# A preactivation convolution pair on one core: the high and low f16 planes move into one buffer, pixel by pixel side by side

## The reference

```python
x = x + silu(bn(sum_e routing[b, e] * conv3x3(gn(x), w_experts[e])))   # 4 experts, routing = sigmoid(mean(gn(x)) @ w_route.T + b_route)
x = x + conv3x3(gn(x), sign(W))                                       # all weights are -1, 0 or 1
```

## Time and profile before

| | |
|---|---|
| median of three runs | 274.24 us (274.05 to 274.51) |
| the profiled execution | 273.91 us |
| its span in the trace | 272.1 us |
| TensorE busy | 264.7 us, 97% of the span, 1339 matmul records |
| VectorE busy | 256.2 us, 94% |
| ScalarE busy | 219.7 us, 81% |
| GpSimd busy | 54.1 us, 20% |
| granted TensorE clock, mean | 0.998 |

### The profile page before, as it was taken

The page is one execution under the profiler, slowest core; times in us unless marked ns, Lnnn a source line. Parts: engine busy times, 40 slices in busy tenths (PEclk is TensorE's granted clock), DMA queues, the critical chain, the costliest instruction groups (busy, mean ns, idle before and its releaser), DMA issues.

```text
span 272.1 us, 4138 instructions
## 1 busy us (share of the span) xinstructions
PE 264.7 (97%) x1339; PEld 181.9 (67%) x1339; DVE 256.2 (94%) x466; ACT 219.7 (81%) x450; POOL 54.1 (20%) x63
## 2 busy tenths in 40 slices
PE   8899999999999999999999999999999999999993
PEld 7545846768485766859586675848576685958663
DVE  5799999999999999999999999999999999996985
ACT  2489998998969898897989899897989986835870
POOL 3001020312131031414112041413203141210110
PEclk9999999999999999999999999999999999999999
DMA  6988855452715555351645544362555536182407
GB/s 200 416 356 281 316 184 154 73 128 50 136 78 87 147 78 143 57 111 78 111 123 77 154 65 93 90 123 96 81 154 77 122 66 125 77 137 96 77 2 154
DMA packets 10245, 35.20 MB, mean 129 GB/s; under 512 B 1264, under 2 KB 1904, under 8 KB 10224
## 3 DMA queue, kind: packets, MB, share of 16 engines
q0 software_dynamic: 4176, 15.21, 33.1%
q1 hardware_dynamic: 5616, 19.34, 18.7%
q10 hardware_dynamic: 432, 0.39, 0.4%
HBM read 11.34 MB, written 16.25 MB: 101 GB/s over the span
## 4 chain that ended last, share of the span: by engine, by line
PE 92%; DMA 2%; DVE 2%; ACT 1%; SPq 1%; issue 1%; POOL 0%; DVEq 0%
PE pc L590 42%; PE pa L555 15%; PE pb L555 14%; PE pe_ L555 13%; PE pd L545 6%; DMA X<-x 2%; PE ps L524 1%; PE ps L528 1%; PE pa L627 0%; PE pb L627 0%; DVE U L1152 0%; DVE X L1377 0%; ACT hi L929 0%; SPq L408 0%; POOL rstd L441 0%
## 5 line engine op out<-in xcount | busy, mean ns | idle before, releaser
L1162 DVE SCALAR_TENSOR_TENSOR U<-we,route,U 128x1152 f32<-128x1152 f32 x45 | 63.6, 1414 | 0.6
L590 PE MATMUL pc<-hi,ws 128*128 128x496 f16 (+3 forms) x270 | 59.8, 375 | 0.5 <-ACT hi L929 0.5
L590 PE MATMUL pc<-lo,ws 128*128 128x496 f16 (+3 forms) x270 | 59.7, 375 | 0.0
L441 POOL TENSOR_TENSOR rstd<-ve,nhalf 128x2 f32<-128x2 f32 (+1 forms) x19 | 26.6, 1399 | 135.0 <-ACT ve L844 111.3
L590 PEld LDWEIGHTS pc<-hi,ws 128*128 128x128 f16 x270 | 26.4, 98 | 30.0 <-issue 0.9
L590 PEld LDWEIGHTS pc<-lo,ws 128*128 128x128 f16 x270 | 26.5, 102 | 27.8
L555 PE MATMUL pa<-V,UM 128*128 128x256 f32 (+1 forms) x180 | 41.7, 381 | 0.0
L555 PE MATMUL pb<-V,UM 128*128 128x256 f32 (+1 forms) x180 | 40.7, 376 | 0.1
L555 PE MATMUL pe_<-V,U 128*128 128x256 f32 (+1 forms) x180 | 40.6, 375 | 0.0
L555 PEld LDWEIGHTS pb<-V,UM 128*128 128x128 f32 x180 | 34.0, 190 | 5.4 <-issue 0.6
L555 PEld LDWEIGHTS pe_<-V,U 128*128 128x128 f32 x180 | 34.1, 190 | 3.8
(11 more groups left out here) (165 smaller groups left out, 394.8 us busy)
## 6 DMA issues: line engine op xcount, KB each, us to landing
X<-x SPq DMA_DIRECT2D x15, 512.0 KB, 5.6
out<-X SPq DMA_DIRECT2D x15, 512.0 KB, 2.6
out<-ev POOLq DMA_DIRECT2D x15, 512.0 KB, 5.4
X<-y POOLq DMA_DIRECT2D x14, 512.0 KB, 4.5
we<-w_experts SPq DMA_DIRECT2D x2, 768.0 KB, 8.9
ws_raw<-w_sign SPq DMA_DIRECT2D x1, 576.0 KB, 11.5
we<-w_experts SPq DMA_DIRECT2D x1, 512.0 KB, 6.8
out<-X SPq DMA_DIRECT2D x1, 384.0 KB, 2.7
```

The source lines that it names most:

```text
L441: g.tensor_tensor(rstd[:, c, a:b], ve[:, c, a:b], nhalf[:, a:b], ALU.pow).then_inc(rstd_ready, 1)
L590: mm = mm_(rows[:, r0 - first // W:r1 - first // W, c0:c1], ws[:, tap * C:(tap + 1) * C], plane((hi, lo)[part], i)[:, r0 + ky - 1:r1 + ky ...
L1162: v.scalar_tensor_tensor(out=nine(U[i % RING]), in0=expert(e), scalar=route[:, i, e:e + 1], in1=nine(U[i % RING]), op0=ALU.mult, op1=ALU.a ...
```

## The change

The four buffers hi0, hi1, lo0 and lo1 become two, hilo0 and hilo1, of as many pixels and two f16 numbers for each pixel. hi and lo are the first and the second number of each pair. The bytes are as many as before; every instruction, its order, its waits and its number of elements stay. What differs is that each instruction that reads or writes hi or lo now steps by two f16 elements (four bytes) from pixel to pixel, where it stepped by one (two bytes).

```diff
         last_size = LAST_TILES * POINTS * W + LAST_REST * W
-        hi = [sb(f"hi{p}", [C, HW if p != (B - 1) % 2 else last_size], F16) for p in range(2)]
-        lo = [sb(f"lo{p}", [C, HW if p != (B - 1) % 2 else last_size], F16) for p in range(2)]
+        hilo = [sb(f"hilo{p}", [C, HW if p != (B - 1) % 2 else last_size, 2], F16) for p in range(2)]
+        hi = [hilo[p][:, :, 0] for p in range(2)]
+        lo = [hilo[p][:, :, 1] for p in range(2)]
```

## The result

The changed kernel takes 279.38 us (median of four runs, 278.99 to 279.60) against 274.34 us for the kernel before in the same session: a ratio of 1.0187, with an interval of 1.0174 to 1.0199. It is slower, as forecast, but by 5.0 us and not by 112. The case that came true is the second rival, a smaller loss, in its second form: the reading side lost a part.

A forecast was written before the change was run, and what follows sets the result against it. TensorE, without gaps, was taken to bound the kernel. Terms of +108.0 (sign products), +4.3 (last image) and -0.5 us (a vanished wait) made +111.8, forecast 386.0 us; range for eight in ten 273.7 to 390.

The forecast's parts named there:

- the second rival: Slower writes, 286 us at most, or sign products losing part of their pace, 1.1 us per 1%; chance 0.09.
- The bound: Whole kernel: TensorE has no gap, so whatever lengthens a sign product lengthens the 15.60 us step by as much.
- What fits both rows is one word per partition every two cycles: TensorE's operand reads: four bytes every two cycles, inferred from f32 pace and f16 rows of 31 costing as much as 32.
- the upper end: Sign products on TensorE: one column in two cycles, so eighteen take 7.41 us instead of 3.81.
- the term of +108.0 us: Sign products of images 0 to 14: two runs of eighteen per image, each 3.60 us longer.
- The tail: Last image: two slower product runs before the inverse transform, +1.83 us, and VectorE waiting for pe_, +2.5; together +4.3 us.
- The term of -0.5 us: Last image: TensorE's 0.47 us wait for ScalarE's statistics goes, as longer sign products let them come in time.
- The writes: ScalarE writing hi, VectorE writing lo: a four-byte pitch costs nothing; upper estimate each row again, hidden if TensorE slows.
- The cover of 0.36 us: Between ScalarE's end of hi at 113.87 and TensorE's use at 114.23: slack that hides slower writing of hi.
- its 0.31 us of the earlier trace: VectorE's slack in each step: it may grow by 0.31 us before it matters, covering slower writing of lo.
- sign_points: Three VectorE sums using lo may lose their fast form, 0.6 us once, hidden in a 2.73 us wait for pa.
- No change: TensorE's reading side takes any two pixels in one beat, sign products keep their time: 274.2 us; chance 0.26.

The follow-up runs named there:

- the planes apart: Kernel before with 10 KB per partition freed, plus hi and lo each at a four-byte pitch in a buffer of its own: 279.06 us, ratio 1.0179.
- the first of the two programs with single streams: Separate program, no kernel changed: streams of one instruction form at several pitches; 512 f16 columns took 216 ns packed, 226 at 4 bytes, 451 at 8.

## Why the prediction was wrong, by its own steps

**The bound was read rightly.** TensorE sets the step, has no gap, and what a sign product gains in length the step gains 36 times.

**The step that failed** is the one that ends "What fits both rows is one word per partition every two cycles", and with it the choice of the upper end, "a sign product runs at the f32 pace". Two facts of the trace were joined that have nothing to do with each other. The f32 products' pace, two cycles a column, was taken for the pace of memory; it is not, for f16 at the same pitch takes 226 ns (L77) where 512 f32 columns take 429 (L112). A row of 31 f16 pixels does cost as much as one of 32, but two pixels need not lie in one word to come at full pace. In place of words the runs showed lines of 16 bytes, 1.76 ns each. The 18 products touch 12 x 128 + 6 x 120 = 2256 lines (a row of 31 or 32 pixels has 8), 3.97 us, and the chain has 3.98. So the term of +108.0 us measured +5.0. The error would have shown at once if the f32 row had been used as what it was, a bound from above, with nothing in the rows to say how far below it the truth lay; half of the chance and more went to its far end.

**The tail** of +4.3 us hung on the same step.

```profile
268.17 1.01 PE pb L628 x12
269.18 1.03 PE pa L628 x12
...
273.42 0.36 DVE X L1387
```

Here the products of L628 have 48 lines, 84 ns, against 82 to 83 before: two runs of 1.01 and 1.03 us for 0.99 and 1.01. From the start of pb's run to VectorE's last instruction it is 5.25 us for 5.22, and VectorE still sets the end. The term of -0.5 us, which counted on a longer run of sign products, measured -0.1: TensorE's wait for the statistics (L506, at 262.36) is 0.36 us for 0.47.

**The writes** were taken at zero, because f32 neighbours with the same pitch are as fast. That comparison missed that f32 fills its words. A half-word written into a word costs, and each hi took 0.30 us more, each lo 0.16. The cover of 0.36 us from the earlier trace rows was right and held all but some 0.3 us in total. VectorE had its 0.31 us of the earlier trace rows and did not come up.

**sign_points** went as written: three sums slower by 0.2 us, hidden by VectorE's wait for pa, which was 2.10 us (L1238) for 2.73.

**The rivals.** No change, with 0.26, failed by 4%: the reading side does take two pixels from two words in a beat, as that rival had it, but the supply of lines falls just short, 225 ns for 216. The rule that was named beside it, of the Trainium skill, "Advanced Engine Details and Errata", section Memory Cachelines, has the right unit, lines of 16 bytes, and the wrong threshold for this engine at full clock: by it a line needs at least two hits, and, as the prediction read it, two suffice; here four hits cost 4% and two (8 bytes, 451 ns) more than double the time. The measurement decides. The smaller loss came true by its second form: 4.4% on the sign products (3.98 for 3.81 us) at the 1.1 us for each 1% that it gave is 4.9 us. What was missing was a way to size it, and the program with one pitch after another gives it. This case had a chance of 0.09. That the range of 273.7 to 390 holds the measured time is luck: it was stretched down to no change for another rival's sake, and the likeliest case by itself was 382 to 390.

What stays open: lo took 1383 ns in the changed kernel and 1314 with the planes apart, while VectorE alone shows no price for reading and writing halves of the same words (1293, and 1340 for the costliest pattern). The 70 ns lie under cover; their cause was not looked for.

## What to carry to other kernels

Count the 16-byte lines that a moving operand touches and hold 1.76 ns for each against the time of its columns: packed f16 uses half of that supply (64 lines, 113 of 216 ns), a 4-byte pitch slightly more than all of it, and each further byte of pitch up to 16 is paid in full. Interleave by whole lines (rows of 64 bytes cost nothing here), not by elements, and never write half-words where the writer is on the path. When the trace of before does not have an operation, a neighbour with another type bounds its price but does not set it.

## What the runs showed of the hardware that was not expected

The supply of lines does not follow TensorE's clock. In the first of the two programs with single streams, the stretches (us, TensorE busy, granted clock) of L85, of L87 and of the f32 products (L112 to L116) were:

```profile
88.00:104.00 16.00, 16.00 (x25) 0.57 0.00 0
104.00:125.00 21.00, 21.00 (x25) 0.50 0.00 0
...
199.00:242.00 43.00, 43.00 (x76) 1.00 0.00 0
```

At pitches of 12 and 16 bytes the clock was granted at 0.57 and then 0.50 of full, which is 1.2 GHz, though matmuls stood back to back throughout; a line still took 1.76 ns (676 / 384 and 900 / 512). The f32 products at 16 bytes took the same 899 ns a record at the full clock, so the lines come at one pace at either clock. A TensorE that waits for its operand is busy in the profile; in f16 it yet lost its clock at pitches of 12 bytes and more, in f32 at the same price it kept it. Why the two differ was not looked for. Every pixel has a line of its own already at 16 bytes, and at 32 bytes (L89, (147.69 - 125.66) / 24 = 918 ns) the price hardly changes.

A line written in half-words costs 4.4 ns on ScalarE, more than twice a line of whole words (1998 / 1024, under 2 ns). It was the same for two half-words in a line (L141) and for one (the first program, at 16 bytes).
